# Moving one PSUM refill of an attention unit: the maxima's second pair of banks goes between the first two refills of the exponentials

## The reference

```
x = x + tanh(g_xattn) * cross_attention(layernorm(x), ctx)
x = x + tanh(g_ffn)   * mixture_of_experts(layernorm(x))
```

```
attn = softmax(q @ k.T)                    # 800 x 2888 for each head
attn = round(attn / (rowmax(attn)/255)) * (rowmax(attn)/255)
out  = attn @ v
```

## Time and profile before

| | |
|---|---|
| median of 3 runs | 1150.7 us (1149.89 to 1155.46) |
| the profiled execution's own time | 1151.49 us |
| its span, first to last instruction | 1149.9 us |
| PE matmuls busy | 976.2 us, 85% |
| VectorE busy | 650.7 us, 57% |
| ScalarE busy | 509.0 us, 44% |
| GpSimd busy | 461.7 us, 40% |

### The profile page before, as it was taken

The page is one execution under the profiler, slowest core; times in us unless marked ns, Lnnn a source line. Parts: engine busy times, 40 slices in busy tenths (PEclk is TensorE's granted clock), DMA queues, the critical chain, the costliest instruction groups (busy, mean ns, idle before and its releaser), DMA issues.

```text
span 1149.9 us, 16600 instructions
## 1 busy us (share of the span) xinstructions
PE 976.2 (85%) x5718; PEld 522.0 (45%) x5719; DVE 650.7 (57%) x1140; ACT 509.0 (44%) x1072; POOL 461.7 (40%) x352
## 2 busy tenths in 40 slices
PE   6999998777777777777777768999999999999993
PEld 3334443233333333433343334655556566565651
DVE  5876676677777777777777755482111111111146
ACT  2022222388878887888788854211122121212110
POOL 1053343056667767676566650017111111111155
PEclk9999999899999999999999988899999999999996
DMA  9921333577888878778566544305363655564145
GB/s 333 196 103 75 106 101 100 128 136 146 171 163 163 183 170 163 170 175 162 110 116 107 87 80 158 156 37 189 135 219 141 219 206 180 195 226 141 55 140 156
DMA packets 264496, 172.45 MB, mean 150 GB/s; under 512 B 239344, under 2 KB 239344, under 8 KB 262128
## 3 DMA queue, kind: packets, MB, share of 16 engines
q1 hardware_dynamic: 250016, 124.67, 45.2%
q0 software_dynamic: 14416, 46.94, 11.7%
HBM read 68.67 MB, written 44.63 MB: 99 GB/s over the span
## 4 chain that ended last, share of the span: by engine, by line
PE 41%; POOL 28%; issue 15%; DVE 10%; DMA 3%; ACT 1%; POOLq 0%; SPq 0%; DVEq 0%; ACTq 0%
POOL arena_a L1343 24%; PE ps L684 16%; PE ps L704 9%; PE ps L553 5%; PE ps L530 5%; POOL expert_in L1355 2%; PE ps L654 2%; POOL expert_in L1347 2%; PE ps L714 1%; DVE v_q L1264 1%; PE ps L695 1%; DVE proj_i L1003 1%; PE ps L512 1%; DVE amax L997 1%; DVE proj_d L1014 1%
## 5 line engine op out<-in xcount | busy, mean ns | idle before, releaser
L1043 DVE TENSOR_REDUCE span_max<-ps 128x1 f32<-128x481 f32 (+2 forms) x400 | 351.6, 905 | 94.3 <-PE ps L570 81.1
L858 ACT ACTIVATE arena_a<-ps,exp_bias,q_step 128x962 uint8<-128x962 f32 (+1 forms) x288 | 331.5, 1157 | 91.1 <-PE ps L570 63.6
L1343 POOL CAST arena_a<-arena_a 128x3072 bf16<-128x3072 uint8 x100 | 274.7, 2747 | 182.3 <-DMA arena_a<-arena_a 181.9
L570 PE MATMUL ps<-arena_a,q_t 128*128 128x481 bf16 (+1 forms) x864 | 207.6, 372 | 87.5 <-ACT arena_a L858 49.8
L684 PE MATMUL ps<-arena_a,xt 128*128 x544 | 172.3, 460 | 1.8 <-issue 1.8
L570 PEld LDWEIGHTS ps<-arena_a,q_t 128*128 128x128 bf16 x864 | 71.8, 98 | 195.6 <-ACT arena_a L858 85.3
L1202 DVE TENSOR_TENSOR proj_d<-ps,proj_f 128x352 f32<-128x352 f32 x48 | 25.2, 524 | 204.2 <-ACT proj_f L893 204.2
L704 PE MATMUL ps<-arena_a,proj_r 128*128 (+3 forms) x288 | 133.6, 600 | 0.7 <-ACT proj_r L899 0.7
L899 ACT COPY proj_r<-ps 128x128 f32<-128x128 f32 x144 | 28.4, 270 | 227.2 <-PE ps L695 227.2
L684 PEld LDWEIGHTS ps<-arena_a,xt 128*128 128x128 f32 x544 | 100.7, 190 | 61.0 <-issue 17.8
L570 PE MATMUL ps<-arena_b,q_t 128*128 128x481 bf16 (+1 forms) x288 | 69.0, 369 | 27.9 <-ACT arena_a L858 17.1
(11 more groups left out here) (168 smaller groups left out, 965.3 us busy)
## 6 DMA issues: line engine op xcount, KB each, us to landing
arena_a<-in_w_up SPq DMA_DIRECT2D x18, 1408.0 KB, 6.3
arena_a<-in_w_down SPq DMA_DIRECT2D x18, 768.0 KB, 8.5
key_parts<-parts SPq DMA_DIRECT2D x23, 512.0 KB, 2.6
expert_in<-proj_r POOLq DMA_DIRECT2D x42, 256.0 KB, 2.9
xt<-expert_in POOLq DMA_DIRECT2D x36, 256.0 KB, 2.9
expert_out<-xt POOLq DMA_DIRECT2D x34, 256.0 KB, 2.3
arena_a<-in_ctx_t SPq DMA_DIRECT2D x3, 1536.0 KB, 14.2
expert_out<-proj_r POOLq DMA_DIRECT2D x17, 256.0 KB, 3.4
```

Source lines behind the costliest of these rows:

```text
L570: last = mm(ps[:, bank + b, 0:w], q_t[:, head, t * P:(t + 1) * P], k_t[head % NK][:, a:a + w], start=True, stop=True)
L858: nc.scalar.activation(halves[:, :, a:a + w], ps[:, bank:bank + 2, 0:w], ACT.Exp, bias=exp_bias[:, n % 2:n % 2 + 1], scale=step_of, accum_ ...
L1043: v.tensor_reduce(span_max[:, n % 2, j:j + 1], ps[:, bank:bank + len(blocks), 0:w], AX.XY, ALU.max).then_inc(s_max, 1)
L1343: p.tensor_copy(p_t[n % NPT].rearrange("p c q -> p (c q)").rearrange("p (j i) -> p j i", j=2), pt_u8[n % NT8].rearrange("p (i j) -> p j i" ...
```

## The change

In PE's loop, M2 of tile n moves from behind E1 of tile n-1 to before it. No instruction is added or removed on any engine, no semaphore or bank changes, and only PE's order differs.

```
             for n in range(NTILE + 4):
                 if n >= 2:
                     for_exp(n - 1, 0)
+                for_max(n, 2)
+                if n >= 2:
                     for_exp(n - 1, 1)
-                for_max(n, 2)
                 for_max(n, 3)
                 if n == 4:
                     pe.wait_ge(s_vq, 16 * (NG - 1))
                 if n == (NG - 1) * GT + 4:
                     pe.wait_ge(s_vq, 16 * NG)
                 weigh_values(n - 4)
                 for_max(n + 1, 0)
                 for_exp(n - 1, 2)
                 for_max(n + 1, 1)
```

## The result

The changed kernel takes 1084.7 us (median of 4 runs, 1084.66 to 1087.04), against 1152.7 us (1149.89 to 1155.46) for the kernel before: a ratio of 0.9415, with an interval of 0.9385 to 0.9446. The table of the kernel before has 1150.7 for three executions; 1152.7 is the median with a fourth, run beside the changed kernel. The forecast was 1086, in a range of 1064 to 1116. The profiled execution took 1084.69 us, with a span of 1083.1.

What follows compares the result with a forecast made beforehand. The prediction took a ring of waits among PE, ScalarE and VectorE, 4.57 us a tile, as the bound. Savings of 35.8 us in 59 tiles and 28.7 in 37, together 64, took 1150.7 to 1086, range 1064 to 1116.

Steps and rivals of the forecast that it cites:

- The ring of 4.57: Attention loop: PE, ScalarE and VectorE wait on each other, 4.57 us a tile; moving M2 before E1 cuts it.
- the ring's four terms: A2's release 1.30, E1 and M2 to X2 1.03, X2 to M0's release 1.21, M0 and E2 to A2 1.03.
- The next limit, 3.76: Attention loop after the cut: period falls from 4.57 to 3.76 us, by 0.81, without a limit from elsewhere.
- the three-engine ring: PE, ScalarE and VectorE waiting on each other after the cut: 7.51 us over two periods, or 3.76 each.
- The zero-write stretch at 4.00: Tiles 8 to 66: DMA work of 3.76 us at 0.95 busy, plus the tail's share, gives 4.00 us a tile.
- The sum: Attention saving: 35.8 us from 59 tiles with zero writes plus 28.7 from 37 others, 64 us in all.
- Rival 1: Attention transfers stay hidden, DMA share of 0.82 being no limit: 78 us gained, 1073 (1065 with small gaps recovered); chance 0.24.
- Rival 2: DMA engines give little more than today in the attention: 1109 if they stop at 0.88, 1115 at 0.85; chance 0.24.
- Rival 3: Nothing changes: conversion and transpose are the true ring, the attention period stays 4.57, 1150 us; chance 0.04.
- Rival 4: Slower: M2, waiting for VectorE before E1, delays E1, A1 and A2; 4.75 a tile, 1165 us; chance 0.04.

Runs made afterwards that it cites:

- before_zeros_early: The kernel before the change, with its zero writes issued during the key projections instead of in the attention; 1154.3 us, ratio 1.0022.
- nokeys: The changed kernel without the attention's 56 key pieces, every head using the keys of the first two; 1078.1 us, ratio 0.9340.
- nokeys_zeros_on_sp: nokeys with the zero writes issued by SP behind each transpose instead of by GpSimd behind each conversion; 1068.5 us.
- w_later: The changed kernel with W one tile later in PE's order, a fourth widened buffer and ScalarE's output copy one tile later; 1090.1 us.
- zeros_early: The changed kernel with its 59 zero writes issued during the key projections and none in the attention; 1071.7 us, ratio 0.9315.
- m2_first: zeros_early with M2 one place earlier still in PE's order, before E0; 1088.5 us.
- E0: Not a run: a group of matmuls in PE's attention loop, which m2_first puts behind M2.

## Why the prediction came out right

- **The ring of 4.57 and its cut** held. The undisturbed turn went from 4.57 to 3.67, the ring's four terms close on the old number, and before_zeros_early shows that the zero writes had no part in it. M2 goes at X0's end, and E1 0.61 after M2's start; the working had 3.62 - 3.05 = 0.57.
- **The next limit, 3.76,** was 0.09 too high, by two small terms. VectorE starts X2 0.07 before the bias has ended (3.67, not 3.74), and W holds PE for 0.60, not 0.75 (7.51 becomes 7.36, 3.68 a turn). VectorE's own work is the limit now; ScalarE has some 0.1 us of room, and the three-engine ring is no more than 0.01 above VectorE.
- **The zero-write stretch at 4.00** measured 3.977, but that it came so near was luck. I took fixed work of 3.76 us a tile and engines that could be 0.95 busy. They were 0.99 busy, and the same work took them longer: 78.1% and 20.6% of 3.977 from 270 to 470 us is 3.93. With the first correction alone the forecast would be 3.76 / 0.99 = 3.80, with the second alone 3.93 / 0.95 = 4.13; the two errors cancel. And the share passed 1 in other runs, so 0.95 was no ceiling. What is shown is that DMA work makes this stretch longer than 3.7: without the zero writes the turns are 3.736, with twice as many 4.566. That it matters who issues the writes and when, beside their amount, is shown by nokeys against nokeys_zeros_on_sp (3.858 and 3.723 at the same share); the prediction did not have it. How much of the 0.3 us is capacity and how much too few buffers stays open, since w_later only moved the wait.
- **The sum**: 35.8 us forecast for the 59 tiles, 36.9 measured; 28.7 forecast for the other 37, 28.6 measured in the other 39 (5.5 + 7.1 + 16.0). Inside the latter two misses cancel, which is luck too: tiles 67 to 80 were slower than 3.83 (4.081), the last faster (3.691).
- **Rival 1** (transfers hidden, 1073) did not occur with the zero writes in place. It comes near with them moved away (zeros_early, 1072), though there the turns are 3.736 and not its 3.80. By the Trainium skill (Perfetto Trace Analysis, "Identifying the Most-Contended Engine") 16 engines make DMA occupancy misleading. Here a share of 0.83 before the change did foretell trouble from the DMA, but not its size: nokeys at 0.86 has turns of 3.858 and zeros_early at 0.84 of 3.736.
- **Rival 2** had the mechanism but too low a ceiling; the engines gave 0.99. (Its second number is off by its own terms: at 0.85 they give 1117, not 1115.) **Rival 3** is out, by the timeline. **Rival 4** did not occur: the cause it names, an M0 held by a W that waits for GpSimd, did appear in the zero-write stretch, but the lag did not grow from tile to tile: 35 of the 59 turns stayed below 3.76. m2_first shows the rival's kind one place further on: behind M2, E0 comes late and costs 17 us.

## What to carry to other kernels

When engines in a ring each idle a little, add up the ring from the timeline until it closes on the period, then do the same for the rings that remain; the smallest edit that cuts the largest one is worth the distance to the next. Before trusting that number, multiply the DMA share by the old period over the new: here 0.83 x 4.57 / 3.67 = 1.03, and transfers that nobody but GpSimd waited for before held up the new loop. Look at the odd tile too: here one in 25 has a W that costs 0.74 us more. Take the time that an instruction group holds an engine from start to next start, not from the row's duration.

## What the runs showed of the hardware

- The same DMA transfers delayed the transposes more when GpSimd issued them behind its conversions than when SP issued them behind the transpose on its own queue: median landings 4.4 against 3.7 at equal shares (0.86 and 0.87), 10 us of the kernel. By the Trainium skill (DMA: Bandwidth & Descriptors, "Queues, rings and completion order") each engine takes packets of its queues in turn. The landings agree with that, but the moment of issue differs too, and the order of packets was not read.
- Engine time of fixed DMA work is not fixed. From 270 to 470 us the transposes, key pieces and zero writes of a tile took 3.79 us of 16 engines at a share of 0.83 and 3.93 at 0.99. The share is not bounded by 1: it went up to 1.08 with double zero writes.
- 24 matmuls with a weight load each hold PE for 0.60 us when they are 32 columns wide (row duration 0.75) and for 1.34 us when they are 128 wide (row duration 1.50).
